# The high half of y made by ScalarE instead of VectorE

## The reference, cut to what matters

```python
h = (x - mu) * jax.lax.rsqrt(var + EPS) * ln_gamma + ln_beta
y = h @ w1 + fc1_bias          # w1: 512 x 2048, dequantised by groups of 128 rows
y = jax.nn.silu(y)
z = y @ w2 + fc2_bias          # w2: 2048 x 512, dequantised by groups of 128 rows
g = silu(residual + 0.5 * z)
```

## Time and profile before

| what | value |
|---|---|
| median of 3 runs | 1339.03 us (1338.12 to 1340.52) |
| the profiled execution | 1339.37 us, its span 1337.6 us |
| granted TensorE clock, mean over the span | 0.977 of full speed |
| TensorE matmul busy | 1225.3 us, 92% |
| VectorE busy | 1121.2 us, 84% |
| ScalarE busy | 1075.0 us, 80% |
| GpSimd busy | 382.0 us, 29% |

### The profile page before, as it was taken

How to read it: one execution, slowest core, us unless ns; L and a number is a source line. 1 busy time by engine, 2 the same in 40 slices (tenths; PEclk the granted TensorE clock), 3 DMA queues, 4 the chain that set the end, 5 groups by cost and what they waited for, 6 DMA issues and landing times.

```text
span 1337.6 us, 19050 instructions
## 1 busy us (share of the span) xinstructions
PE 1225.3 (92%) x6144; PEld 633.7 (47%) x6144; DVE 1121.2 (84%) x1894; ACT 1075.0 (80%) x1885; POOL 382.0 (29%) x465
## 2 busy tenths in 40 slices
PE   1279999999999999999999999999999999999994
PEld 0034454545545454554545455454545545454551
DVE  5978798888979888897988889798888979888774
ACT  1349888888888888888888888888888888888885
POOL 4115241321414132141413214141422314142111
PEclk8579999999999999999999999999999999999998
DMA  9201021120302112030211203021120303011011
GB/s 327 54 2 32 1 57 40 32 64 2 93 1 64 32 33 64 5 91 0 65 31 33 64 12 84 1 75 21 33 63 15 82 1 82 14 36 29 18 46 32
DMA packets 38837, 61.21 MB, mean 46 GB/s; under 512 B 9553, under 2 KB 9809, under 8 KB 38737
## 3 DMA queue, kind: packets, MB, share of 16 engines
q1 hardware_dynamic: 38448, 59.87, 17.4%
q10 hardware_dynamic: 288, 0.08, 0.0%
HBM read 43.14 MB, written 16.78 MB: 45 GB/s over the span
## 4 chain that ended last, share of the span: by engine, by line
PE 67%; DVE 19%; issue 6%; ACT 6%; POOL 1%; DMA 1%; SPq 0%; DVEq 0%; ACTq 0%; POOLq 0%
PE blk L421 26%; PE blk L438 22%; PE side L382 9%; DVE blk L630 7%; PE side L406 3%; DVE y_lo L641 3%; ACT blk L525 2%; PE side L370 2%; DVE g_lo L610 2%; DVE y_hi L636 2%; ACT y_full L518 2%; PE side L359 1%; DVE g_rows L605 1%; ACT h_full L484 1%; DVE fin L657 1%
## 5 line engine op out<-in xcount | busy, mean ns | idle before, releaser
L630 DVE TENSOR_SCALAR blk<-blk,ratio 128x512 f32<-128x512 f32 x768 | 572.5, 753 | 177.7 <-PE blk L421 172.9
L525 ACT ACTIVATE blk<-blk,ratio 128x512 f32<-128x512 f32 x960 | 625.7, 667 | 73.5 <-PE blk L438 66.6
L421 PE MATMUL blk<-h_hi,q_sb 128*128 128x512 f16 x1024 | 391.7, 383 | 73.2 <-DVE blk L630 35.9
L421 PE MATMUL blk<-h_lo,q_sb 128*128 128x512 f16 x1024 | 390.4, 381 | 0.0
L438 PE MATMUL blk<-y_hi,w_sb 128*128 128x512 f16 x1024 | 388.9, 380 | 0.0
L438 PE MATMUL blk<-y_lo,w_sb 128*128 128x512 f16 x1024 | 388.6, 380 | 0.0
L518 ACT ACTIVATE y_full<-blk,par,last 128x512 f32<-128x512 f32 x256 | 199.3, 779 | 41.3 <-PE blk L421 41.3
L641 DVE SCALAR_TENSOR_TENSOR y_lo<-y_full,up,y_hi 128x512 f16<-128x512 f32 x256 | 228.3, 892 | 0.1
L938 POOL TENSOR_TENSOR out_sb<-fin,s_rows 128x512 f32<-128x512 f32 x62 | 80.2, 1294 | 446.4 <-ACT fin L537 443.1
L421 PEld LDWEIGHTS blk<-h_hi,q_sb 128*128 128x128 f16 x1024 | 100.3, 98 | 218.7 <-DVE blk L630 102.6
L923 POOL TENSOR_TENSOR h_lo<-h_full,h_hi 128x512 f16<-128x512 f32 x64 | 86.8, 1356 | 388.2 <-DVE h_hi L614 373.9
(11 more groups left out here) (132 smaller groups left out, 1151.2 us busy)
## 6 DMA issues: line engine op xcount, KB each, us to landing
xt<-in_x SPq DMA_DIRECT2D x64, 256.0 KB, 4.8
x_again<-in_x SPq DMA_DIRECT2D x256, 64.0 KB, 1.9
out<-out_sb SPq DMA_DIRECT2D x256, 64.0 KB, 1.7
w_sb<-in_q SPq DMA_DIRECT2D x4, 1024.0 KB, 13.8
zt<-in_q SPq DMA_DIRECT2D x2, 1024.0 KB, 15.4
y_hi<-in_q SPq DMA_DIRECT2D x1, 1024.0 KB, 10.1
y_lo<-in_q SPq DMA_DIRECT2D x1, 1024.0 KB, 12.3
s_rows<-in_wqkv SPq DMA_DIRECT2D x1, 768.0 KB, 7.9
```

What stands on the lines that cost most here:

```text
L421: mm = pe.matmul(blk[J % 2][:], q1_sb[:, g, j // 4, w, j % 4 * P:(j % 4 + 1) * P], a[:, c % 2, g, :], start=(g == 0 and n == 0), stop=(g = ...
L525: act.activation(blk2[hb][:], blk2[hb][:], ACT.Copy, scale=ratio2[:, KC * j + hb:KC * j + hb + 1]).then_inc(blk2_scaled, 1)
L630: dve.tensor_scalar(blk[J % 2][:], blk[J % 2][:], ratio1[:, at:at + 1], None, ALU.mult).then_inc(blk_scaled, 1)
```

## The change

`y_high` moves from VectorE's queue to ScalarE's. It stays in the slot after the silu; in ScalarE's loop it stands behind `block2_out`, the fc2 rescale of that slot. It is now an activation (copy with the pointer scale `up_y`) instead of a tensor_scalar, with the same input and output. `y_low` stays on VectorE in its place and waits for `y_hi_done` as before. Since `up_y` is made on VectorE, a new semaphore `y_scaled` is raised behind it by a copy of one column, and ScalarE waits for it once, before block 0.

```diff
+            def y_high(J):
+                if J == 0:
+                    act.wait_ge(y_scaled, 1)
+                act.wait_ge(silu_done, J + 1)
+                wait(act, blk2_done, KC * (J - Y_RING + 1))
+                act.activation(y_hi[:, J % Y_RING, :], y_full[:, J % 2, :], ACT.Copy, scale=up_y
+                               ).then_inc(y_hi_done, 1)
...
                 if at := fc2_step(G):
                     block2_out(*at)
+                if G >= 1 and (at := fc1_step(G - 1)) and at[1] == KC - 1:
+                    y_high(at[0])
...
-            def y_high(J):
-                dve.wait_ge(silu_done, J + 1)
-                wait(dve, blk2_done, KC * (J - Y_RING + 1))
-                dve.tensor_scalar(y_hi[:, J % Y_RING, :], y_full[:, J % 2, :], up_y, None, ALU.mult
-                                  ).then_inc(y_hi_done, 1)
...
+            dve.tensor_copy(mix[:, 1:2], up_y).then_inc(y_scaled, 1)
             dve.tensor_scalar(b2_half[:], b2_c, 0.5, None, ALU.mult).then_inc(z_bias_done, 1)
...
-                if G >= 1 and (at := fc1_step(G - 1)) and at[1] == KC - 1:
-                    y_high(at[0])
                 if G >= 2 and (at := fc1_step(G - 2)) and at[1] == KC - 1:
                     y_low(at[0])
```

More of the change, by code:

```diff
@@ L222, in build @@
         q2_quarter, top_q2_done, top_q2_known = sem("q2_quarter"), sem("top_q2_done"), sem("top_q2_known")
-        q2_scaled, z_bias_done = sem("q2_scaled"), sem("z_bias_done")
+        q2_scaled, z_bias_done, y_scaled = sem("q2_scaled"), sem("z_bias_done"), sem("y_scaled")
         h_scales, s1_scaled, q1_scale, wqkv_split = (
```

## The result

| | before | changed |
|---|---|---|
| median | 1338.72 us (4 runs, 1338.12 to 1340.52) | 1393.73 us (4 runs, 1392.96 to 1394.52) |
| ratio | | 1.0409, 95% interval 1.0391 to 1.0427 |
| span of the profiled execution | 1337.6 us | 1392.3 us |
| granted TensorE clock, mean | 0.977 | 0.964 |

The change costs 55 us, 4.1%. The page of the changed kernel: busy times, the granted clock in 40 slices, and the chain that ended last by line.

The account below looks back on a forecast made before the run. TensorE, 92% busy, was taken as the bound, with only its gaps to gain. +1.9 us a chunk, 27 over fourteen, plus first chunk, last chunk and start gave +30 us: 1369 us; stated range 1327 to 1400, the forecast's own 1350 to 1388.

Parts of the forecast that it names:

- rival (d): ScalarE finds no room at all, six of eight short intervals full: 1402 us, from 1388 up; chance 0.20.
- slot 54, silu only: New activation moves this slot's silu by 0.62 us; TensorE loses only about 0.1 us a chunk.
- slot 59, y_lo waits for y_hi: y_lo, queued ahead of the rescale TensorE needs, waits for ScalarE's y_hi: +0.56 us a chunk.
- slot 62, late silu: y_hi of block 59 goes ahead of the silu that TensorE's next chunk waits for: +0.62 us.
- silus of slots 6 and 30: Short full ScalarE intervals, slots 3 to 6 and 27 to 30, delay the even silus: +0.6 us for both.
- slot 17, qk_t behind y_hi: y_hi comes ahead of qk_t, for which the scores product waits: +0.25 us a chunk.
- slot 42: Bare stretch where y_hi comes late and y_lo stands ahead of the rescales: +0.15 us, once per chunk.
- the gain: VectorE's relief at two places a chunk, around slots 34 and 48 to 52: -0.35 us.
- Rival (b): VectorE's relief wins, ScalarE's backlog staying within silu's room and y_lo not held: 1312 to 1336 us; chance 0.22.
- The first and the last chunk: First: three full ScalarE intervals, 1.9 us; last, without turns: 1.0 us; the start's added column copy: 0.15 us.

Follow-up runs that it names:

- guard: The changed kernel, with GpSimd's h_lo waiting for the y_lo of the same slot, so y_lo is never behind it: 1373.9 us.
- relief: The kernel before, with y_hi never written by any engine and y_lo waiting for the silu instead: 1329.7 us, ratio 0.993.
- act_load: The kernel before, VectorE still making y_hi, plus an equal activation on ScalarE into a spare tile nobody reads: 1371.2 us, ratio 1.023.
- even_act: The changed kernel with only even blocks' y_hi on ScalarE, the odd blocks' back on VectorE: 1357.0 us, ratio 1.013.

## Why the prediction was right, and where its sizes were off

The sign held, and so did the mechanism as far as it went: ScalarE's queue got late and y_lo became a wait of its own. The size didn't: +30 us were forecast, +55 measured. The time, 1393.7, is above the forecast's own range, which ended at 1388. It lies in the stated range, 1327 to 1400, only because that took in the lower half of rival (d), whose mechanism isn't what happened; that part is luck. By its steps, for a chunk without a fall of the clock:

| step | forecast | measured |
|---|---|---|
| slot 54, silu only | +0.1 | 0 |
| slot 59, y_lo waits for y_hi | +0.56 | +1.31 |
| slot 62, late silu | +0.62 | +0.62 |
| silus of slots 6 and 30 | +0.6 | +0.31 |
| slot 17, qk_t behind y_hi | +0.25 | +0.41 |
| slot 26, r_t behind y_hi | not seen | +0.48 |
| slot 42 | +0.15 | +0.10 |
| the gain | -0.35 | -0.28 |
| sum | +1.93 | +2.95 |
| the clock | not seen | +0.8 to 1.0 in 8 of 14 chunks |

**Slot 62** went as worked out; its silu (L518), with TensorE's product behind it, in the chunk of 80.57 us:

```profile
312.95 0.80 ACT L518 ACTIVATE y_full<-blk,par,last 128x512 f32<-128x512 f32 x1
...
313.81 0.39 PE L421 MATMUL blk<-h_hi,q_sb 128*128 128x512 f16 x1 [0.72 <-ACT y_full L518]
```

**Slot 17** was the right wait. One y_hi takes 0.73 there, and qk_t, pushed to 822.35, comes after the product wants it, at +0.41 for the slot: it starts 822.88 - 821.68 = 1.20 us after its slot, where it had been 791.29 - 790.42 = 0.87. That is 0.33 of the 0.41; the other 0.08 lies behind it, between the scores product and the next fc1 product (0.30 us for 0.22).

```profile
821.74 0.73 ACT L526 ACTIVATE y_hi<-y_full,up 128x512 f16<-128x512 f32 x1
...
822.35 0.39 ACT L502 ACTIVATE qk_t<-side 128x256 f32<-128x256 f32 x1
...
822.88 0.46 PE L391 MATMUL side<-qk_t 128*128 128x128 f32 x2 [0.17 <-ACT qk_t L502]
```

**Slot 59** (58 in the counts above) is the term that was mis-sized: forecast +0.56, measured +1.31. I had y_lo wait for y_hi, hold the rescale for 0.56 and keep its own 0.75 us. Late by so little, it is overtaken by h_lo: 0.87 more, as guard shows. I even had the two durations of the earlier trace rows and the mean of y_lo, 892 ns against 0.75, in view, and didn't ask what makes some y_lo long. The rest agrees: guard's +0.46 against my 0.56.

**The gain** was about what was forecast, and relief shows why it's small: at the stops VectorE's queue holds g_lo, h_hi and y_lo, which are released late, and y_hi isn't what is in front of them. Rival (b), in which the relief wins, needed up to 27 us of it with hardly any cost on ScalarE. relief, which had all of the relief and no cost, gained 10 of them, and act_load, with the cost alone, lost 31.5. The silu of slot 54 moves by 0.47 us against its slot (0.79 to 1.26), where (b) needed less than about 0.2.

**The first and the last chunk** together with start and end were to cost 1.9 + 1.0 + 0.15; by the chunks' starts they cost 3.2 and 3.4. Some of that is the clock: the changed kernel has a fall at 145.8 and one at 1374.6 that the kernel before doesn't have. With 14 chunks of +2.95 and 8 falls of 0.85 that makes 41.3 + 6.8 + 6.6 = 54.7, the difference of the spans. So of the 25 us that I was short, 14 are in the chunks' own sum, 7 in the clock, and 3.5 at the two ends.

**What the profile was to show.** ScalarE was to be over 92% busy from 149 us on; it is 989.45 of 1086 us, 91%. y_hi was to take 0.68 to 0.72 us; it takes 0.74. But what it holds up, from its start to the next one's in a full queue, is 0.61 in the median, as the forecast's 0.62 had it. TensorE's wait for the silu over 3 us a chunk, y_lo idle for y_hi, the stop above 1.5 and VectorE near 75%: 3.1, 1.4, 2.46 and 76%. By the chunk the busy sums were both off: VectorE 63.5 us where 58 was forecast, ScalarE 73.6 where 75.8 was. Busy time counts the overlap of neighbours once, so 16 y_hi of 0.54 us don't take 8.7 off: relief, with y_hi away altogether, is still at 61.1, 5.7 less than before. That the total cost resembles rival (d), which has no room anywhere, is an accident: the long intervals do drain the queue (slots 11, 19, 27 and 35 have no late silu), and only one of the eight short intervals, before slot 62, costs more than 0.2.

**Small slips in the sums.** From 842.24 to 842.89 is 0.65 us and not 0.63, so the silu ends at 1.43 of 1.72 us and has 0.29 of room. Six times 0.6 and the 0.8 of rival (d) are 4.4 a chunk and not 4.2, which would put it at 1405. Neither moves the forecast.

## What to carry to other kernels

Before moving work to an engine with room on the average, go through its queue in order and ask of each instruction behind the new one who waits for it; here the instructions behind it (qk_t, r_t and the even silus above all) cost 1.9 us a chunk where the relieved engine gave 0.5. An instruction that only has to be done in the next several slots, like y_lo, doesn't belong ahead of one that TensorE waits for two slots later: moving it saved 19 us, where taking its neighbour away altogether saved 10. And a small delay can change who comes first at something that two engines share, so look for instructions whose longest and median durations lie far apart.

## What the runs showed of the hardware

**VectorE and GpSimd hold each other up.** y_lo takes 1.62 and 1.74 us for 0.75 where h_lo's record starts 0.09 us before it or 0.04 after, and h_lo takes 1.59 for 1.15 where y_lo's starts 0.16 or 0.17 ahead. Kept apart (guard) they take 0.75 and 1.15. The one that is ahead isn't slowed: h_lo keeps its 1.15 while y_lo stands. The Trainium skill, "SBUF — State Buffer", section "SBUF: two separate sides", says that VectorE, in an instruction with two SBUF inputs, and GpSimd, in one that reads SBUF, want the same port pair, and that whoever starts first has it until its instruction ends. The runs agree up to a constant: in the changed kernel h_lo has 1.06 us to go when y_lo starts, and y_lo is 0.87 too long; in act_load y_lo has 0.59 to go and h_lo is 0.44 too long. All 72 long y_lo of the changed kernel, behind h_lo or out_sb, are too long by what was left of GpSimd's instruction less 0.20 us, within 0.01. Not every overlap costs: where y_lo starts 0.32 us behind GpSimd's `v`, once a chunk, it keeps its 0.75, and no run here shows why. And where the records start within 0.05 us of each other they don't tell who wins: 0.043 to 0.045 ahead, y_lo lost in 13 chunks of even_act; 0.048 ahead, it won in one.

**A longer stop brought the clock down.** With stops of 0.40 to 1.60 us ahead of slot 59 the granted clock stayed at 1.00 in all 14 middle chunks of a run. With 2.07 it fell after 3 of 13, with 2.46 after 8 of 14. In the first chunk, which isn't among these, stops of 1.99 at the same place were followed by a fall in 5 of 6 runs, and shorter ones, 0.89 to 1.70, in none of 4. In the changed kernel's chunk shown above it was 0.78 over the window from 876.00 to 876.50 and 0.50 for the 3 us behind that, so it fell some 0.6 us after TensorE had started again at 875.69. In the other chunks the fall came between 0.2 us before TensorE's restart and 1.3 us after it. The two matmuls of a slot are then 0.43 us apart instead of 0.22, and a fall costs 0.8 to 1.0 us of a chunk, in even_act 1.4. What decides whether it falls after a given stop, these runs don't tell.
